# The 64-row rests of two down projections on the two row halves of the array

## What is computed

```python
# WKV(x, w, u): a decaying sum over time of exp(k)*k and of exp(k), forward and backward,
# num/den, times sigmoid(x), times a scale per batch; k is fside_BxSxS_0 (4, 256, 256)

# layer 0: y = WKV(x, ...), flattened to 1024 tokens
logits = y @ router                              # 8 experts, top 2 per token, softmax over the two
buf    = scatter tokens into (8, 320, 256)       # capacity 320 per expert; overflow is dropped
g, u   = split(buf[e] @ w_up_gate[e], 2)         # 176 hidden units per expert
out[e] = (silu(g) * u) @ w_down[e]               # 176 -> 256
routed = gather out by token, weighted
g, u   = split(y @ shared_w_up_gate, 2)          # 704 hidden units
shared = (silu(g) * u) @ shared_w_down           # 704 -> 256
x = x + routed + shared

# layer 1: h = WKV(x, ...)
x = x + relu(h @ W_up.T) @ W_down.T + sum(softmax(top2(h @ W_gate.T))) * (h @ W_expert)
```

## Time and profile before

| | |
|---|---|
| runs | 178.53, 180.38, 178.94 us, median 178.94 |
| profiled execution | 179.44 us, of which the profile spans 177.7 us |
| PE matmul / weight load | 144.6 us (81%) / 117.6 us (66%) |
| DVE, ACT, POOL busy | 134.6, 71.2, 69.2 us |
| granted TensorE clock | 0.987 of 2.4 GHz in the mean |
| chain that ended last | PE 40%, DVE 33%, issue 9%, DMA 7%, POOL 7% |

### The profile page before, as it was taken

How to read it: one execution, slowest core, us unless ns; L and a number is a source line. 1 busy time by engine, 2 the same in 40 slices (tenths; PEclk the granted TensorE clock), 3 DMA queues, 4 the chain that set the end, 5 groups by cost and what they waited for, 6 DMA issues and landing times.

```text
span 177.7 us, 2207 instructions
## 1 busy us (share of the span) xinstructions
PE 144.6 (81%) x666; PEld 117.6 (66%) x666; DVE 134.6 (76%) x293; ACT 71.2 (40%) x168; POOL 69.2 (39%) x83
## 2 busy tenths in 40 slices
PE   0000297799999969995999999899999977999992
PEld 0000285688898858883777877677788856878781
DVE  0899979999998996724499969967589434787624
ACT  3699374454053005223427534623633201232330
POOL 5388022732487770560050050050002577762130
PEclk9999999789999999999999999999999999999998
DMA  4999999995002320129702072012104033332111
GB/s 96 255 340 369 395 413 258 194 279 200 1 31 96 111 87 32 37 48 331 281 1 74 3 221 74 30 44 76 61 17 148 30 116 90 112 101 89 59 59 59
DMA packets 14843, 23.61 MB, mean 133 GB/s; under 512 B 1974, under 2 KB 10375, under 8 KB 14704
## 3 DMA queue, kind: packets, MB, share of 16 engines
q1 hardware_dynamic: 13296, 19.49, 35.1%
q0 software_dynamic: 1536, 3.99, 7.1%
HBM read 15.29 MB, written 8.39 MB: 133 GB/s over the span
## 4 chain that ended last, share of the span: by engine, by line
PE 40%; DVE 33%; issue 9%; DMA 7%; POOL 7%; ACT 2%; SPq 0%; DVEq 0%; POOLq 0%; ACTq 0%
PE hb L833 23%; PE dn L833 10%; DVE euk L647 9%; POOL ek L403 4%; DVE df L604 4%; DVE nf L604 3%; PE tp L847 3%; DVE euk L639 2%; DMA buf<-slots_in 2%; DMA ekv<-slots_out,get_at 2%; DMA cond_s<-cond 2%; POOL ekv L403 2%; PE tp L923 2%; PE dk L833 2%; DVE df L597 1%
## 5 line engine op out<-in xcount | busy, mean ns | idle before, releaser
L833 PE MATMUL hb<-xc,sup_s 128*128 128x256 f32 x176 | 43.1, 404 | 2.3 <-DVE hid L684 2.3
L833 PEld LDWEIGHTS hb<-xc,sup_s 128*128 128x128 f32 x176 | 35.3, 204 | 8.2 <-DVE hid L684 3.1
L492 ACT ACTIVATE gate_a<-hb 128x256 f32<-128x256 f32 (+3 forms) x40 | 16.1, 403 | 35.5 <-PE hb L833 28.3
L343 POOL TENSOR_TENSOR euv<-euv,nf 128x512 f32<-128x512 f32 x6 | 7.8, 1296 | 55.6 <-DVE nf L604 55.6
L833 PE MATMUL hb<-bufT,mup_s 128*112 128x320 f32 (+1 forms) x96 | 27.3, 434 | 1.0 <-issue 0.5
L647 DVE RECIPROCAL euk<-euk 128x256 f32<-128x256 f32 x16 | 26.8, 1714 | 0.0
L847 PE MATMUL tp<-turn,xc 128*128 128x136 f32 x32 | 5.5, 325 | 22.4 <-DVE xc L656 22.4
L833 PEld LDWEIGHTS hb<-bufT,mup_s 128*112 128x112 f32 (+1 forms) x96 | 17.1, 181 | 9.1 <-issue 1.7
L833 PE MATMUL dn<-mdn_s,hidm 112*128 112x256 f32 x96 | 22.1, 380 | 0.0
L833 PE MATMUL dn<-sdn_s,hid 128*128 128x256 f32 x96 | 21.7, 381 | 0.1
L355 POOL DMA_INDIRECT slots_in<-htok,put_at x16 | 16.3, 1019 | 10.2 <-DVE put_at L729 5.8
(11 more groups left out here) (107 smaller groups left out, 203.1 us busy)
## 6 DMA issues: line engine op xcount, KB each, us to landing
mup_s<-mup SPq DMA_DIRECT2D x4, 704.0 KB, 15.3
slots_in<-outb SPq DMA_DIRECT2D x10, 256.0 KB, 9.2
slots_out<-outb SPq DMA_DIRECT2D x8, 256.0 KB, 2.2
buf<-slots_in SPq DMA_DIRECT2D x4, 384.0 KB, 4.7
k<-k_cm SPq DMA_DIRECT2D x4, 256.0 KB, 3.8
xc<-x_cm SPq DMA_DIRECT2D x4, 256.0 KB, 8.3
sup_s<-sup SPq DMA_DIRECT2D x2, 512.0 KB, 8.7
xt<-x_tm SPq DMA_DIRECT2D x1, 1024.0 KB, 11.0
```

The costliest lines, as they stand in the source:

```text
L343: nc.gpsimd.tensor_tensor(euv[:, n % 2], euv[:, n % 2], nf[:], ALU.add).then_inc(num_ready[n], 1)
L492: nc.scalar.activation(dst, src, ACT.Silu).then_inc(silu_ready, 1)
L833: return nc.tensor.matmul(dst, w, m, start=first, stop=last)
```

## The change

- The rest of the shared hidden units goes to a new tile `tail`: tokens 0 to 127 on partitions 0 to 63 and tokens 128 to 255 on partitions 64 to 127. DVE writes it with two multiplications in place of one. The rest rows of `sdn` are loaded twice, once to each half of the partitions.
- The experts' rest goes to `hidt` in the same way: slots 0 to 255 on partitions 0 to 63, slots 256 to 319 on 64 to 127. `mdn`'s rest rows are loaded twice, to the halves of `mdn_t`.
- `shared_down` makes the five full products of each tile first, tile i into bank `dn[i]`, and then the two rest products: 64 rows of the array each, on the lower and the upper half, into the two banks. Both banks are now used for each batch, so the products of batch b wait until DVE has taken batch b-1. For batch 3 both rest products stand behind the second tile.
- `expert_down` makes three products of 112 rows and then three of 64 rows: tiles 0 and 1 on the lower row half into `dn[0]`, tile 2 on the upper one into `dn[1]`. It waits for both copies of the expert before at its start.
- `take_shared` reads the first 256 columns of two banks in place of the 512 of one.
- Of the six zero fills two remain: the unused slots of `hidm` (112 partitions, 128 elements) and of `hidt` (64 partitions, 128 elements).

```diff
--- before.py
+++ after.py
@@ -84,17 +84,20 @@
         turn = sb("turn", [P, CH, P + E])
         sup_s = sb("sup_s", [P, CH * 2 * J])
         sdn_s = sb("sdn_s", [P, NCHUNK, C])
+        tail = sb("tail", [P, 2, P])
         mup_s = sb("mup_s", [P, E, CH, 2 * I])
-        mdn_s = sb("mdn_s", [IA, E, 2, C])
+        mdn_s = sb("mdn_s", [IA, E, C])
+        mdn_t = sb("mdn_t", [P, E, C])
         ident = sb("ident", [P, P])
         before = sb("before", [P, P], BF16)
         ones = sb("ones", [P, P], BF16)
         iota_e = sb("iota_e", [P, E])
         gate_a = sb("gate_a", [P, 2, CAP])
-        hid = sb("hid", [P, 2, NCHUNK, T])
+        hid = sb("hid", [P, 2, JC, T])
         buf = sb("buf", [P, 2, 5, C])
         bufT = sb("bufT", [P, 2, CH, 2 * CAP])
-        hidm = sb("hidm", [IA, 2, 2, SLOT_TILES * P])
+        hidm = sb("hidm", [IA, 2, SLOT_TILES * P])
+        hidt = sb("hidt", [P, 2, 2 * P])
         outb = sb("outb", [P, 2, 3, C])
 
         zero = outb[:].rearrange("p k r d -> p (k r d)")[:, 0:512]
@@ -131,7 +134,8 @@
             return ctx.enter_context(nc.psum_tensor(name, [P, 512], F32))
 
         hb = [bank(f"hb{i}") for i in range(3)] + [bank("dk")]
-        dn = [bank(f"dn{i}") for i in range(2)]
+        dnn = ctx.enter_context(nc.psum_tensor("dn", [P, 2, 512], F32))
+        dn = [dnn[:, i] for i in range(2)]
         tp = [bank(f"tp{i}") for i in range(2)]
 
         decay = hb[3][:, 0:2 * B * CH].rearrange("p (l b c) -> p l b c", l=2, b=B)
@@ -265,7 +269,8 @@
                 sp.dma_start(sup_s[:, a:z], sup[:, a:z]).then_inc(ld_sup[i], 16)
             sp.dma_start(xc[:, 2], x_cm[:, 2]).then_inc(ld_x[2], 16)
             sp.dma_start(sdn_s[:, 0:JC], sdn[0:JC * P].rearrange("(j p) d -> p j d", p=P)).then_inc(ld_sdn, 16)
-            sp.dma_start(sdn_s[0:JR, JC], sdn[JC * P:J]).then_inc(ld_sdn, 16)
+            for at in (0, JR):
+                sp.dma_start(sdn_s[at:at + JR, JC], sdn[JC * P:J]).then_inc(ld_sdn, 16)
             sp.dma_start(xc[:, 3], x_cm[:, 3]).then_inc(ld_x[3], 16)
             sp.dma_start(xt[:], x_tm).then_inc(ld_xt, 16)
 
@@ -278,8 +283,9 @@
                 sp.dma_start(mup_s[:, 2 * q:2 * q + 2], mup[:, 2 * q:2 * q + 2]).then_inc(ld_mup[q], 16)
 
             load_mup(0)
-            sp.dma_start(mdn_s[:, :, 0], mdn[:, 0:IA].rearrange("e i d -> i e d")).then_inc(ld_mdn, 16)
-            sp.dma_start(mdn_s[0:IB, :, 1], mdn[:, IA:I].rearrange("e i d -> i e d")).then_inc(ld_mdn, 16)
+            sp.dma_start(mdn_s[:], mdn[:, 0:IA].rearrange("e i d -> i e d")).then_inc(ld_mdn, 16)
+            for at in (0, IB):
+                sp.dma_start(mdn_t[at:at + IB], mdn[:, IA:I].rearrange("e i d -> i e d")).then_inc(ld_mdn, 16)
             for q in range(1, E // 2):
                 load_mup(q)
 
@@ -372,7 +378,7 @@
             values(0)
             bonus(0, 0)
             values(1)
-            pads = (hid[JR:P, :, JC], sdn_s[JR:P, JC], hidm[IB:IA, :, 1], mdn_s[IB:IA, :, 1], hidm[0:IB, :, 1, CAP:], hidm[:, :, 0, CAP:])
+            pads = (hidt[IB:P, :, CAP - 2 * P:P], hidm[:, :, CAP:])
             pool.wait_ge(ekv_ready, 2)
             for i, pad in enumerate(pads):
                 nc.gpsimd.memset(pad, 0.0).then_inc(padded, 1)
@@ -672,23 +678,32 @@
                     if j < JC:
                         up, g, dst = banks[0][:, T:2 * T], gate_a[:, c % 2, 0:T], hid[:, b % 2, j]
                     else:
-                        up, g, dst = banks[0][0:JR, 0:T], gate_a[0:JR, c % 2, 0:T], hid[0:JR, b % 2, j]
+                        halves = ((0, 0, P), (JR, P, T))
+                        src, to = (banks[0][0:JR], gate_a[0:JR, c % 2]), tail[:, b % 2]
                 else:
                     e = b
                     if e >= 2:
                         v.wait_ge(mo_ready, 2 * (e - 1))
                     if j == 0:
-                        up, g, dst = banks[1][0:IA, 0:CAP], gate_a[0:IA, c % 2], hidm[:, e % 2, 0, 0:CAP]
+                        up, g, dst = banks[1][0:IA, 0:CAP], gate_a[0:IA, c % 2], hidm[:, e % 2, 0:CAP]
                     else:
-                        up, g, dst = banks[0][0:IB, 0:CAP], gate_a[0:IB, c % 2], hidm[0:IB, e % 2, 1, 0:CAP]
-                nc.vector.tensor_tensor(dst, up, g, ALU.mult).then_inc(hid_ready, 1)
+                        halves = ((0, 0, 2 * P), (IB, 2 * P, CAP))
+                        src, to = (banks[0][0:IB], gate_a[0:IB, c % 2]), hidt[:, e % 2]
+                if j < (JC if kind == "shared" else 1):
+                    nc.vector.tensor_tensor(dst, up, g, ALU.mult).then_inc(hid_ready, 1)
+                else:
+                    for at, a, z in halves:
+                        last = nc.vector.tensor_tensor(to[at:at + JR, 0:z - a], src[0][:, a:z], src[1][:, a:z], ALU.mult)
+                        if at == 0:
+                            tick(last)
+                    last.then_inc(hid_ready, 1)
 
             def take_shared(b):
                 v.wait_ge(sh_ready, b + 1)
                 if b == 0:
                     v.wait_ge(ld_xt, 16)
                 t = xt[:, b * TB:(b + 1) * TB]
-                nc.vector.tensor_tensor(t, dn[b % 2][:].rearrange("p (n d) -> p n d", n=TB), t, ALU.add).then_inc(sh_taken, 1)
+                nc.vector.tensor_tensor(t, dnn[:, :, 0:C], t, ALU.add).then_inc(sh_taken, 1)
 
             def route(r):
 
@@ -865,21 +880,20 @@
 
             def shared_down(b, tiles=range(TB)):
                 if b == 0:
-                    pe.wait_ge(ld_sdn, 32)
-                    pe.wait_ge(padded, 6)
+                    pe.wait_ge(ld_sdn, 48)
                 last_chunk = chunks.index(("shared", b, JC))
                 pe.wait_ge(hid_ready, last_chunk)
-                if b >= 2:
-                    pe.wait_ge(sh_taken, b - 1)
-                if b == B - 1:
+                if 1 <= b < B - 1:
+                    pe.wait_ge(sh_taken, b)
+                elif b == B - 1:
                     pe.wait_ge(mo_taken, 2 * E)
                 for i in tiles:
-                    for j in range(NCHUNK):
-                        if j == JC and i == 0:
-                            pe.wait_ge(hid_ready, last_chunk + 1)
-                        last = mm(dn[b % 2][:, i * C:(i + 1) * C], hid[:, b % 2, j, i * P:(i + 1) * P], sdn_s[:, j],
-                                  j == 0, j == NCHUNK - 1)
-                if i == TB - 1:
+                    for j in range(JC):
+                        mm(dn[i][:, 0:C], hid[:, b % 2, j, i * P:(i + 1) * P], sdn_s[:, j], j == 0, False)
+                if tiles[-1] == TB - 1:
+                    pe.wait_ge(hid_ready, last_chunk + 1)
+                    for i in range(TB):
+                        last = mm(dn[i][:, 0:C], tail[i * JR:(i + 1) * JR, b % 2], sdn_s[i * JR:(i + 1) * JR, JC], False, True)
                     last.then_inc(sh_ready, 1)
 
             def ranks(r):
@@ -939,14 +953,18 @@
             def expert_down(e):
                 if e == 0:
                     pe.wait_ge(sh_taken, B - 1)
-                    pe.wait_ge(ld_mdn, 32)
+                    pe.wait_ge(ld_mdn, 48)
+                    pe.wait_ge(padded, 2)
                 pe.wait_ge(hid_ready, nearly + 2 * e + 2)
+                if e >= 1:
+                    pe.wait_ge(mo_taken, 2 * e)
                 for r in range(SLOT_TILES):
-                    if e >= 1 and r != 1:
-                        pe.wait_ge(mo_taken, 2 * (e - 1) + (1 if r == 0 else 2))
-                    for j in range(2):
-                        last = mm(dn[r // 2][:, (r % 2) * C:(r % 2 + 1) * C], hidm[:, e % 2, j, r * P:(r + 1) * P],
-                                  mdn_s[:, e, j], j == 0, j == 1)
+                    nc.tensor.matmul(dn[r // 2][:, (r % 2) * C:(r % 2 + 1) * C], hidm[:, e % 2, r * P:(r + 1) * P], mdn_s[:, e],
+                                     start=r != 1, stop=False, skip_group_check=True)
+                for r in range(SLOT_TILES):
+                    row, at = (r // 2) * IB, (r % 2) * P
+                    last = nc.tensor.matmul(dn[r // 2][:, (r % 2) * C:(r % 2 + 1) * C], hidt[row:row + IB, e % 2, at:at + P],
+                                            mdn_t[row:row + IB, e], start=False, stop=True, skip_group_check=True)
                     if r >= 1:
                         last.then_inc(mo_ready, 1)
 
```

## The result

The changed kernel takes 181.97 us in the median of 14 runs (179.42 to 184.73), the kernel before 178.92 us beside it (178.53 to 180.73, 14 runs). The ratio is 1.0095 with a 95% interval of 1.0055 to 1.0136. By the medians of all runs the ratio is 1.017. So the kernel is a little slower, where I forecast 178.8 us and no change, and 181.97 lies past the upper end of my range, 181.7.

What follows compares the result with a forecast made beforehand. DVE was taken to set the pace up to 65.8 us, PE in the expert stage, POOL's gathers behind 139.28. Terms -1.16 + 0.23 + 0.11 + 0.72 + 0 gave -0.1 us, 178.8 us on the median; range 177.1 to 181.7.

Steps and rivals of the forecast that it cites:

- the fills: Dropping four of POOL's zero fills shortens DVE's line 613 near 14 us and line 640: gain 1.16 us, bounds 0 and 1.4.
- the loads hidden: Loading the rest rows of `mdn` and `sdn` twice costs 0, since SP is idle then; without that cover up to 2.8 us.
- the wait before the last expert: Between down(6) and down(7), PE waits 1.0 us for both of ACT's copies of the expert before.
- the store in place of DVE as the gathers' releaser: The last store comes 1.42 us later, 0.7 of it slack, so its landing releases the first gather, 0.72 us past DVE's end.
- the sum for the profiled pair: All terms together, -1.16 + 0.23 + 0.11 + 0.72 + 0 = -0.1 us, against the profiled 179.44 us: 179.3.
- The overlap of a pair: In the down products, neighbouring rest products on different row halves run together: at most one pass of 0.216 us saved per group.
- The switch: PE's change between full and half array, two per group of down products: 0.11 us each, bounds 0 and 0.27.
- the emptying rival: The array empties at each change between full and half array, 0.27 us each: sum +2.3, 181.3 us, slower; chance 0.32.
- s: Net saving per group of down products on PE: 0.216 us less two changes between full and half array; forecast 0.
- DVE's split: Each rest product of DVE made as two instructions costs 0.11 us more: +0.23 before 65.8 us, +0.11 in the expert stage.
- Free switches: Changing between full and half array costs nothing, so each group of down products saves 0.216 us: sum -1.6, 177.3 us; chance 0.21.
- whole overlap without a price: Whole rest products overlap in the down products and changing the array's shape is free, 0.43 us per group: -2.7, 176.2 us; chance 0.05.

## Why the prediction missed

Right: the fills (1.16 us forecast, 1.12 to 1.18 in three comparisons); the loads hidden (18.1 us from the last gated y to the first expert on both sides); the wait before the last expert (1.0 and 1.08); and the store in place of DVE as the gathers' releaser.

**Right by luck:** the sum for the profiled pair, -0.1 us against -0.02. DVE ends its WKV 0.57 us later than forecast (0.25 us of gain in place of 0.82), and because of that the store, forecast 0.72 behind it, is only 0.2 behind: two errors of half a microsecond that cancel at the gathers, with 0.28 us on top that before's execution had lost at its start. And the pair sets an execution of before that is 0.5 us over its median beside the shortest of the changed kernel.

**The step that failed** is the last one of the sum, "Against its own 179.44 us that is 179.3; the profiled execution is 0.5 us over the median, so on the median 178.94 - 0.1 = 178.8 us": it carries a difference between two profiled executions over to the medians and has no term for the granted clock. The changed kernel takes 179.42 us at a clock of 1.000 and 181.97 in the median, at 0.97 to 0.98: some 2.5 us that the sum has nothing for, where before has 0.4 between its shortest run and its median. The line of the clock on before's page had one dip, behind PE's wait of 2.35 us for the fourth chunk's bank (its first row after it starts at 32.25), and I read past it. What the change does to PE's idle times could in part have been read off my own terms. Where DVE leads, it lengthens DVE's share by the splits and shortens PE's: a shared group goes from 5.34 to 5.11 us, by its records. Before `turn_rows(3)` PE's wait grew from 1.49 to 2.14, before the slots from 1.08 to 1.40; before the fourth chunk it grew from 2.35 to 3.58 by the fills alone (3.61 with the fills moved and nothing else). In the profiled execution that did no harm. In the others it did: in the runs at 0.953 the time is 5 us longer than at 1.000. Filling the idle times brought all of eleven runs to 0.997 or more. That idle time lowers the clock is shown; which of the waits does it in which run is not, beyond the traces counted above for the one before `turn_rows(3)`, and the fall is not the same from run to run (before had anything from 0.979 to 1.000 on one chip).

**Mis-sized terms.** The overlap of a pair: 0.43 us, not 0.216. The switch: 0.185 us, not 0.11, between my value and the emptying rival's 0.27. The two errors nearly cancel, s = 0.05 and not 0; that s came out near its forecast is luck as well. DVE's split: 0.29 us, not 0.11. I took it from the slope over columns, which holds for two writes to the same partitions and no more (0.06 measured); the write to the upper partitions was an operation that no row of before shows, and I should have bounded it from both sides. The count was short too: two splits before 65 us, as forecast, but two in the stage and not one, for DVE now holds PE up before the third expert's products as well (0.35 us at 93.33, where PE had not waited). That is 4 x 0.29 = 1.16 in place of 0.34. Together the splits eat the fills' gain.

**The rivals.** The emptying array named almost the time that was measured, 181.3, for a reason that did not hold: its group would have been 2.9 us, and is 2.45. Free switches and whole overlap without a price are out by the same row. None of the rivals had the clock, so the range's upper end was the emptying array's and fell 0.3 us short of the median.

**What remains of the loss.** At full clock, by the traces, the change without its fills costs 1.57 us (177.60 - 176.03): 0.60 before the last gated y and 0.83 from the first expert to the gathers, less 0.04 between them, and 0.18 behind the gathers' start. The splits are 1.16 of it and the later store 0.08; the other 0.3 us are not placed. With the fills' 1.16 this is +0.4; the timed runs at full clock say +0.9 (179.42 against before's shortest, 178.53, whose clock I don't have) to +1.5 (180.16 against 178.6, on another chip). Of the 3.05 us between the medians 0.4 to 1.5 are thus the work itself, and the rest is the lower clock. Below half a microsecond I can't place.

## What to carry to other kernels

Before summing terms, read the line of the granted clock for both sides of the change and list the engine's idle times: a change that makes a matmul stage shorter, where another engine leads, lengthens idle time, and the clock may take back more than the change gives. In the traces here 3.4 us at half clock cost 1.7 to 1.9 us where the rest waited for PE, and 0.04 where DVE led. Where runs of one kernel spread by several per cent, compare times at equal clock first.

A fill, a copy or a load that the change happens to move can be the whole gain. Move it alone: here the kernel before with its fills elsewhere and its waits filled gave 0.9912, and nothing of the half arrays was needed. It was tried on one chip only. On the two where layer 1 stalls it is not shown and, by the nearest version (rest products cut in two by columns, 1.0058), doubtful on one of them; the moved fills alone gave 0.9965 on the other.

Two products on the two row halves do run together, but the array's change of shape costs 0.19 us each way here. One pair per change of shape only just pays; and what makes the operand for the upper half has its own price on the engine that writes it.

## What the runs showed of the hardware that I had not expected

- Matmuls do not always start in the order of issue, if the records are told apart rightly (which tile a record is for is inferred, as said above): a product for the free row half started at 124.393, ahead of one that was issued before it for the busy half (124.916). Its bank was free, and nothing downstream depended on the order.
- A DVE instruction that writes partitions 64 to 127 from partitions 0 to 63 does not overlap with its neighbours: 0.31 us from start to start, against 0.20 for the same shape on the same partitions.
- A memset on POOL of 48 x 2048 elements held up DVE's comparison with a constant (line 613) beside it by 1.07 us (1.39 against 0.32), but not DVE's scan under the same fills, at 12.73 us (1.38 us, and 1.39 in the changed kernel).
- On two of the chips ACT stood still for 7.5 to 13 us during the gathers of layer 1, in every kernel traced there. Its cause is open.
- The same 3.4 us at half clock cost 0.04 us around 33 us and 1.86 us around 67 us of one execution.
